# Window attention after whitening: projecting the next unit's values ahead of the sums of the weights

## The reference

```python
t = xn.reshape(Bb, Cc, WS, n1, WS, n2).transpose(0, 3, 5, 2, 4, 1)
tok = t.reshape(Bb * n1 * n2, WS * WS, Cc)
qk = (tok @ qk_w.T).reshape(-1, WS * WS, 2, HEADS, DH)
q = qk[:, :, 0].transpose(0, 2, 1, 3)
k = qk[:, :, 1].transpose(0, 2, 1, 3)
attn = jax.nn.softmax(jnp.einsum('bhqd,bhkd->bhqk', q, k) * scale, axis=-1)
v = jax.nn.relu(tok @ v_w.T).reshape(-1, WS * WS, HEADS, DH).transpose(0, 2, 1, 3)
o = jnp.einsum('bhqk,bhkd->bhqd', attn, v)
```

## Time and profile before

| | us |
|---|---|
| median of 3 runs | 467.7 (466.11 to 467.86) |
| profiled execution, its time | 465.49 |
| profiled execution, its span | 463.8 |
| PE busy | 428.6 (92%) |
| DVE busy | 362.2 (78%) |
| ACT busy | 271.1 (58%) |
| POOL busy | 192.0 (41%) |

### The profile page before, as it was taken

One profiled execution on the slowest core, in us unless ns is written; L12 is line 12 of the kernel. 1 busy time (PEld: TensorE's weight loads), 2 busy tenths in 40 slices (PEclk: granted clock), 3 DMA queues, 4 the chain that ended last, 5 costly groups with the idle time before them and its releaser, 6 DMA issues. The chain is left out here.

```text
span 463.8 us, 38693 instructions
## 1 busy us (share of the span) xinstructions
PE 428.6 (92%) x17466; PEld 348.4 (75%) x17466; DVE 362.2 (78%) x1151; ACT 271.1 (58%) x455; POOL 192.0 (41%) x158
## 2 busy tenths in 40 slices
PE   7999925797879999999999999999999999999994
PEld 7898825333657888888888888888888888888883
DVE  1586478777457888888888888888888888888884
ACT  3232300577745676666767676766767676767751
POOL 4072000020133555455545555455545554455422
PEclk9999975999999999999999999999999999999998
DMA  8990000010111424334241424334241524334233
GB/s 297 421 397 12 3 1 0 1 53 19 74 54 57 147 89 147 96 113 147 96 139 69 148 86 148 98 114 148 92 139 70 150 84 149 99 116 147 90 105 72
DMA packets 31564, 52.03 MB, mean 112 GB/s; under 512 B 6176, under 2 KB 21024, under 8 KB 30624
## 3 DMA queue, kind: packets, MB, share of 16 engines
q1 hardware_dynamic: 31520, 51.50, 32.9%
HBM read 12.95 MB, written 12.85 MB: 56 GB/s over the span
## 5 line engine op out<-in xcount | busy, mean ns | idle before, releaser
L340 POOL TENSOR_TENSOR X<-X,otok 128x392 f32<-128x392 f32 x63 | 107.7, 1709 | 159.7 <-DVE otok L735 159.7
L695 DVE TENSOR_REDUCE rmax<-ps 113x16 bf16<-113x784 f32 x128 | 124.1, 970 | 44.6 <-PE ps L870 44.6
L908 PE MATMUL ps<-diag,qk_all 64*49 64x98 f32 x4096 | 128.6, 244 | 0.7 <-ACT prob_all L386 0.7
L908 PEld LDWEIGHTS ps<-diag,qk_all 64*49 64x49 f32 x4096 | 105.4, 120 | 23.8 <-issue 23.6
L922 PE MATMUL ps<-mdiag,sel 64*49 64x98 bf16 x2048 | 111.4, 204 | 0.0
L386 ACT ACTIVATE prob_all<-ps 113x784 f32<-113x784 f32 x128 | 105.5, 825 | 6.1 <-PE ps L922 4.4
L334 POOL TENSOR_SCALAR xs<-X,affined 128x392 f32<-128x392 f32 x64 | 70.0, 1094 | 84.5 <-DVE affined L681 56.1
L401 ACT ACTIVATE vst<-ps 49x256 f32<-49x256 f32 x193 | 73.0, 378 | 54.5 <-PE ps L854 52.1
L393 ACT ACTIVATE qk_all<-ps 128x784 f32<-128x784 f32 x64 | 52.7, 824 | 50.4 <-PE ps L834 50.3
L922 PEld LDWEIGHTS ps<-mdiag,sel 64*49 64x49 bf16 x2048 | 62.9, 99 | 0.9
L953 PE MATMUL ps<-prob_all,vst 113*32 113x49 f32 x4096 | 58.8, 208 | 2.8 <-issue 2.8
(11 more groups left out here) (155 smaller groups left out, 393.6 us busy)
## 6 DMA issues: line engine op xcount, KB each, us to landing
diag<-qk_all SPq DMA_DIRECT2D x256, 98.0 KB
out<-X SPq DMA_DIRECT2D x30, 392.0 KB, 4.2
X<-x_in SPq DMA_DIRECT2D x7, 1024.0 KB, 16.3
X<-x_in SPq DMA_DIRECT2D x7, 544.0 KB, 16.9
X<-x_in SPq DMA_DIRECT2D x4, 256.0 KB, 3.6
out<-X SPq DMA_DIRECT2D x2, 294.0 KB, 3.8
X<-x_in SPq DMA_DIRECT2D x2, 192.0 KB, 4.5
out<-X SPq DMA_DIRECT2D x2, 98.0 KB, 3.3
```

What stands on the lines that cost most here:

```text
L340: g.tensor_tensor(rows_of(u), rows_of(u), otok[u % 2][:].rearrange("p k a s -> p k s a"), ALU.add).then_inc(S["x_ready"], 1)
L695: v.tensor_reduce(rmax[u % 3][0:ROW, :, 8 * k:8 * k + 8], ps[0:ROW, B_S:B_S + 2, 0:8 * POS].rearrange("p h (v q) -> p h v q", q=POS), AX.X ...
L908: ins = mm(ps[64 * e:64 * e + POS, B_ST + hh, col:col + 2 * POS], qk[u % 3][r, g, k, 2 + x_, :], diag[u % 3][r, e::2, g, k, x_, :], start= ...
```

## The change

In `rest`, the values of the next unit are projected ahead of the sums of the weights instead of behind them. Nothing else is altered: no instruction is added or left out, and each engine but PE keeps its order.

```diff
                 if has(s):
                     scores_for_max(s, 0)
+                if has(s):
+                    project_v(s)
                 if has(z):
                     sum_weights(z)
                 if has(s):
-                    project_v(s)
                     scores_for_max(s, 1)
                 if has(u):
                     scores_for_exp(u, 1)
```

## The result

The changed kernel takes 481.71 us (median of 4 runs, 479.75 to 484.69) against 467.29 (four runs of the kernel before; the 467.7 further up is the median of three of them): a ratio of 1.0322, 95% interval 1.0272 to 1.0372. A second set of five runs gave 481.39 against 467.58, 1.0292 (1.0275 to 1.0308). So the change costs some 14 us, and the forecast of 480 (474.5 to 485) held.

A forecast was written before the change was run, and what follows sets the result against it. PE was taken to bound the loop, busy in all of its 308 us; 58 rounds x 0.22 us of wait plus a little restart, + 13 us, made 478.5 profiled, 480 as median, range 474.5 to 485.

The forecast's parts named there:

- The wait of 0.22 from round 0: PE waits for ACT's copy before the values, hop 0.18 read from round 0: 0.22 us in 58 rounds, 12.8 us.
- a restart behind the wait: First block after a wait runs slower, weight loads 0.55 against 0.52: at most 58 x 0.03 = 1.7 us more.
- PE's own work unchanged, two and two shape changes: PE enters and leaves the 32-column shape twice a round before and after: both 1.60 us, nothing gained or lost.
- The circle closes on itself: Projection, copy, SP, values, rest of PE's round, next projection: 5.42 us against 5.20, not bought back by earlier starts elsewhere.
- What the hop consists of: From the copy's end by way of SP to the values' first matmul: 0.18 us, taken from round 0.
- lower bound: SP's hop alone, 0.10 us from the copy's end, gives a wait of 0.14, + 8 us.
- Rounds 1 to 3 and 62: Rounds without added wait: other PE stops hide it in 1 to 3, the credit comes early in 62; 58 remain.
- Rival (a), absorbed: The round is DVE's, so PE's wait ahead of the values is absorbed: no change, 465.5 us; chance 0.05.
- Rival (b), faster: No wait, and the earlier second exponential starts PE's scores sooner: 0.03 x 58 = 1.7 us better, 463.8; chance 0.02.
- Rival (c), more behind each stop or a slower clock: Blocks behind each PE stop run slower, 0.1 a round, 484.5 us, or the clock falls, over 600; chance 0.07.
- The signs: Profile after: hole of about 0.2 us ahead of the values with a semaphore as releaser, round 5.42, values to sums 0.58.

The follow-up runs named there:

- experiment 1: Changed order, ACT copying half of the queries and keys from unit 3 on: 466.50 us, 0.9997; the order of before with the same halved copy: 466.23 us, 1.0001.
- experiment 5: Changed kernel with the count-down of qk_kept on the second matmul of the values, not the first: 475.29 us, 1.0163 against the kernel before.
- experiment 3: Kernel before with the sums cut in two halves and the values between them, one more pair of shape changes: 482.76 us, 1.0353.
- both edits: Changed kernel with the credit given by ACT's copy itself and the count-down on the values' second matmul: 473.82 us, 1.0137 against the kernel before.
- experiment 2: Kernel before with PE waiting for the copy's credit ahead of the sums, the values staying behind them: 469.41 us, 1.0052.

## Why the prediction was right, step by step

- *The wait of 0.22 from round 0.* Right: projection to values 2.01 as forecast, 58 x 0.239 = 13.8 us in the loop against 12.8 and a little more. The missing 0.02 a round stand in the stretch from values to projection (3.43, not 3.41). They come with the wait and not with the order, since the same order without it has 3.41 in experiment 1. The forecast had them as the 0.03 for a restart behind the wait, of which it took "a little". Its sign for that, weight loads over 0.55 instead of 0.52, isn't what costs: in the changed kernel of experiment 5 the loads are back at 0.52 and the stretch still has 3.44 (302.48 to 305.92).
- *PE's own work unchanged, two and two shape changes.* Right: 5.197 against 5.208 with the wait out of the way. The price of a pair, 0.24 from starts, was 0.25 to 0.27 when one was added. The Trainium skill, "TensorEngine Tiling (Array Packing)", Key Properties, says that a change of the tiling mode drains the engine; the trace of experiment 3 agrees, with 0.266 us a round for one more pair.
- *The circle closes on itself.* Right: a copy 0.07 longer cost 0.061 a round, a way 0.04 shorter gave 0.037, a form 0.09 shorter 0.093.
- *What the hop consists of.* I put the 0.18 down to the way over SP, and gave SP's part of 0.10 as its lower bound. The number was right and its parts were not: about 0.04 is SP, 0.09 the form of the wait, 0.05 the rest. The 0.10 was no lower bound either, with both edits the hop is 0.05. It did no harm, since the nearest row had the same form; it did in experiment 2, where I carried the 0.18 to a place that had another.
- *Rounds 1 to 3 and 62.* Round 62 has 5.19, no wait, as forecast. That other stops hide the wait in rounds 1 to 3 isn't shown: those rounds vary by more than the wait from profile to profile.
- *Rival (a), absorbed.* Refuted: nothing in the 3.43 gave way. *Rival (b), faster:* its condition never came; with the wait removed by force the order gains 0.011 a round, so its size (0.03) was too large as well. Its place, the 0.71 from the projection to the scores, has 0.71 in the changed kernel too, though the exponential comes 0.16 earlier. *Rival (c), more behind each stop or a slower clock:* refuted. Behind the stop PE takes 0.02 more and not 0.1, and the granted clock in the changed kernel's loop is 1.00, as in the earlier trace rows:

```profile
145.00:470.00 325.00, 321.28 (x14988) 262.32 (x14976) 266.28 (x832) 212.95 (x354) 159.90 (x115) 1.00 0.34 109
```

- *The signs.* One didn't come as described: the hole ahead of the values has no releaser's name, it stands as "issue".

## What to carry to other kernels

Before a block is moved, look up what its wait was hidden behind: a wait that shows nowhere in a profile may be covered by just the block that it is moved past. Here 0.82 us of sums covered a release due 0.22 us after PE would get there. In this chain, which closes on itself, each delay of the release was paid every round, and ACT, freed sooner elsewhere, gave nothing back. A round at the start or the end of a pipeline, where a stage is missing, can show the new order already, with its price: here round 0 did.

## What the runs showed that I had not expected

Where a matmul both waited on a semaphore and counted it down, the wait was a record of its own on PE's sequencer (51 ns), and the matmul started 0.18 us after the end of the copy that released it by way of SP; where it only waited, it started 0.09 after it. This is shown for the values (5.449 to 5.356 a round) and in reverse for the sums (5.246 to 5.326). Why the form costs 0.09 and the record has 0.05 isn't shown. Moving the count-down to the next matmul of the block, with nothing else changed, made the kernel before 1.0% faster (0.9884 to 0.9921), of which the profile places 1.8 of 4.2 us. Whether other engines have the same cost wasn't tried.
